# A perceiver kernel's masked cross attentions: the mask moved from TensorE to DVE and ScalarE

## The chip, the cores and the metric

The kernel runs on one core of one Trainium2 chip. The metric is the device time of one execution in microseconds; the comparison uses the median of several runs. The profile is of one further execution, taken by the hardware profiler.

## The reference, cut to what matters

The input is x, 16 batches of 64 tokens by 256, and a context of 16 x 1601 x 256. Four layers follow each other, each with a cross attention to the context, a second attention (or a scan), and a feed-forward part. Every part adds its result to x. The cross attentions of layers 1 and 3 are masked, those of layers 0 and 2 are not:

```
Q = query @ Wq + bq;  K = ctx @ Wk + bk;  V = ctx @ Wv + bv      # 16 heads of 16
scores = einsum('bhqd,bhkd->bhqk', Q, K) / 4
layer 1:  scores + mask * (-1e9)          # mask (16, 1, 1, 1601), float
layer 3:  where(mask == 0, -inf, scores)  # mask (16, 1601), int
probs = softmax(scores);  out = (probs @ V) @ Wo + bo
```

Everything is float32.

## The kernel before

The program is a sequence of stages with a barrier between them. `refresh` normalises x and projects the queries of the next cross attention; `cross_attention` then runs the attention over the context; other functions hold the other parts. There are four cross attention stages, called x0 to x3 here; in the profile their tiles all bear the name `x_`. x1 and x3 are masked.

In `cross_attention` a *unit* is one group of key tiles for one half of the heads (`c`, 8 heads) of one batch. The 1601 keys are 13 tiles of 128 (the last has 65). `GROUPS` cuts them into 4, 3, 3 and 3 tiles. A batch's context thus takes 8 cycles (`CYCLES`): two halves of the heads by four groups, and a stage has 16 x 8 = 128 cycles with scores and 8 before them. PSUM is two sets of four banks; cycle k works in set k % 2 and the maxima of cycle k are written to the other set. In cycle k, TensorE does, in this order:

- wait for the maxima of the cycle before (`max_done`), then the scores of unit k, keys on partitions (`scores`): a matmul that writes the shift (the negated maximum of every query), then 3 or 4 tiles by 4 banks of 32-row matmuls on top of it. Each bank holds four heads' worth of columns for one of four row groups.
- the scores of unit k+5 a second time with queries on partitions (`maxima`), from which DVE takes the maxima (`take_max`);
- in even cycles the weighted values of earlier units (`weigh`), into bank 0, which ScalarE must have read (`wait_exp(k, 1)`);
- the projection of one or two tiles of values four units ahead (`project_v`), into bank 0 or 1;
- in cycles with k % 4 == 3 a transpose of the maxima into bank 3 (`wait_exp(k, 4)`);
- the projection of the keys of unit k+8 (`project_k`), into bank 1 or 2.

ScalarE takes the exponents of unit k from the four banks (`exponents`), one instruction a bank, splits the context of two batches later into its high part in two cycles of a context (`split_high`), copies the turned shift (`take_shift`) and the projected keys (`take_keys`). DVE takes the maxima, then what was weighed (`take_weighed`), the values (`take_v`), and once a batch it divides and stages queries. POOL computes the low part of the context.

The mask before: `refresh` scales it and splits it into a high and a low part, and SP stores both as two rows a batch in `mask_rows`. `cross_attention` loads these two rows into four row groups of `side`, whose other rows POOL has filled with ones. A matmul over 4 rows (line 516) writes shift plus mask for each tile and bank of the scores, and one over 2 rows (line 544) the mask for each bank of the maxima. SP issues the loads: for every batch both halves of the context (`raw_in`), each after the subtraction that frees its buffer (`low_done`), then, after the last scores of the batch (`s_full`), the mask's rows of two batches later.

Of the kernel before, what the change touches and what calls it, by code (L numbers as in the profile page):

```python
# [13 lines left out]
F32 = mybir.dt.float32  # L14
# [36 lines left out]
class Net:  # L51


    def __init__(self, nc, dram, ctx):
# [11 lines left out]
        self.swap = self.sb("swap", [P, P])  # L66
# [118 lines left out]
def refresh(net, tag, add=None, query=None, xn=None):  # L185
# [3 lines left out]
             "bias_scaled q_ready m_full m_high m_low stored")  # L189
    with ExitStack() as mem, stage(nc, names) as (  # L190
            block, made, biased, added, stats_ready, var_ready, std_ready, rstd_ready, xn_ready, turned, taken, wq_in,
            mask_in, q_full, bias_scaled, q_ready, m_full, m_high, m_low, stored):
# [11 lines left out]
        if query:  # L204
# [4 lines left out]
            m_parts = net.sb(tag + "_mhl", [B, 2, CTX], F32R, ctx=mem) if mask else None  # L209
# [5 lines left out]
        if query:  # L215
            @block.sync
            def _(sp):
# [53 lines left out]
        def _(dve):  # L271
# [40 lines left out]
        def _(act):  # L312
# [10 lines left out]
            for t in range(TILES + LEAD):  # L323
# [15 lines left out]
def cross_attention(net, tag, wk, bk, wv, bv, qT, m_rows, ahead, clear=None):  # L339

    nc, d = net.nc, net.dram
    masked = m_rows is not None
    PADDED = KEY_TILES * P
    WINDOW = 48
    GROUPS = [(0, 4), (4, 7), (7, 10), (10, 13)]
# [7 lines left out]
    names = ("wv_in bias_in raw_in0 raw_in1 wk_high wk_low wv_high wv_low high_done low_done pad_set mask_in0 mask_in1 zero_set side_set shift_set "  # L353
             "sums_set q_staged m_full max_done z_step z_ready z_turned nm_ready s_full exp_done k_full k_taken v_full "
             "v_taken pv_full o_taken o_step out_ready")
    with ExitStack() as mem, stage(nc, names) as (
            block, wv_in, bias_in, raw_in0, raw_in1, wk_high, wk_low, wv_high, wv_low, high_done, low_done, pad_set, mask_in0, mask_in1,
            zero_set, side_set, shift_set, sums_set, q_staged, m_full, max_done, z_step, z_ready, z_turned, nm_ready, s_full,
# [14 lines left out]
        side = net.sb(tag + "_side", [P, 2, PADDED], F32R, ctx=mem) if masked else None  # L373
# [60 lines left out]
        def _(sp):  # L434
# [12 lines left out]
            if masked:  # L447
                sp.wait_ge(side_set, 1)
# [9 lines left out]
            for b in range(B - 2):  # L458
# [3 lines left out]
                if masked:  # L462
                    sp.wait_ge(s_full, CYCLES * b + CYCLES)
# [22 lines left out]
        def _(pe):  # L486
# [18 lines left out]
            def scores(k):  # L505
# [6 lines left out]
                if masked:  # L512
                    for t in range(lo, hi):
                        for j in range(4):
                            r = slice(32 * j, 32 * j + 4)
                            nc.tensor.matmul(mine[j][:, (t - lo) * P:(t - lo + 1) * P], side[r, u, t * P:(t + 1) * P],
                                             nm[r, c], start=(t == lo), stop=True, skip_group_check=(t > lo))
                else:
                    for j in range(4):
                        r = slice(32 * j, 32 * j + 4)  # L520
# [2130 lines left out]
```

## Time and profile before

| | |
|---|---|
| median of 3 runs | 4475.74 us (4473.22 to 4480.47) |
| the profiled execution | 4455.4 us, span 4453.6 us |
| TensorE matmul / weight load | 3800.3 us (85%) / 2972.4 us (67%) |
| DVE | 2224.7 us (50%) |
| ScalarE | 1781.0 us (40%) |
| POOL | 684.8 us (15%) |
| granted TensorE clock, mean | 0.919 of 2.4 GHz |
| DMA | 330.29 MB, mean 74 GB/s |

Busy shares are of the span. PE is TensorE's matmuls, PEld its weight loads (they overlap the matmuls), ACT is ScalarE, SP the engine that issues the loads. The instructions are named by their line in the kernel, by the tile written and the tiles read. "Idle before" is the time in which the engine stood still just before an instruction, and the releaser is what ended that wait; "issue" means that the engine waited for nothing that the profile shows.

### The profile page before, as it was taken

How to read it: one execution, taken by the hardware profiler on the slowest of the kernel's cores; microseconds unless marked ns; L12 is line 12 of the kernel's file. 1: busy time of each engine (PE TensorE's matmuls, PEld its weight loads, DVE VectorE, ACT ScalarE, POOL GpSimd, SP SyncE). 2: the span in 40 equal slices, each digit the busy share in tenths (PEclk: the TensorE clock that was granted, in tenths of full speed). 3: DMA queues.
4: the chain of work that ended last, by engine and by line, in shares of the span. 5: the costliest groups of instructions: out<-in, count | busy, mean ns of one | idle time of the engine just before them, and what ended most of it. 6: DMA issues, size and time to landing. Idle time of an engine off the chain costs nothing. (4 is left out here: it accounts for less than half of the span.)

```text
span 4453.6 us, 141607 instructions
## 1 busy us (share of the span) xinstructions
PE 3800.3 (85%) x64078; PEld 2972.4 (67%) x64078; DVE 2224.7 (50%) x4259; ACT 1781.0 (40%) x3676; POOL 684.8 (15%) x393
## 2 busy tenths in 40 slices
PE   7999998647992799999966889999963789999988
PEld 5777776525771588888725568777843678878865
DVE  4555554542443555555564355555544255555543
ACT  4555453211220345454413345555531244544431
POOL 1111110031005111111140011111112111111100
PEclk9999999668996899999987899999976899999998
DMA  3121210026994211111040111111013611010001
GB/s 102 51 84 58 68 60 12 8 102 241 352 351 133 62 47 35 47 37 45 3 114 2 32 60 47 40 40 47 18 27 140 207 53 48 33 48 33 34 11 33
DMA packets 109045, 330.29 MB, mean 74 GB/s; under 512 B 31680, under 2 KB 55760, under 8 KB 101632
## 3 DMA queue, kind: packets, MB, share of 16 engines
q1 hardware_dynamic: 98800, 299.61, 20.0%
q0 software_dynamic: 6912, 18.88, 1.3%
q8 instruction: 507, 8.31, 0.8%
q10 hardware_dynamic: 2736, 2.75, 0.2%
q14 instruction: 90, 0.74, 0.1%
HBM read 261.80 MB, written 51.00 MB: 70 GB/s over the span
## 5 line engine op out<-in xcount | busy, mean ns | idle before, releaser
L636 DVE TENSOR_REDUCE x_pm<-banks 128x4 f32<-128x1536 f32 (+2 forms) x512 | 935.6, 1827 | 1034.7 <-PE banks L547 1034.7
L759 ACT ACTIVATE x_kT<-banks,x_bk 128x384 f32<-128x384 f32 (+2 forms) x512 | 305.1, 596 | 915.1 <-PE banks L589 915.1
L744 ACT ACTIVATE x_pe<-banks 128x512 f32<-128x512 f32 (+1 forms) x1024 | 474.2, 549 | 194.2 <-PE banks L527 194.2
L576 PE MATMUL banks<-x_wh,x_ch 128*128 128x256 f32 (+1 forms) x1664 | 523.6, 315 | 9.7 <-issue 5.8
L482 POOL TENSOR_TENSOR x_cl<-xnT,x_ch 128x1601 fp32r<-128x1601 f32 x60 | 218.6, 3643 | 1769.5 <-ACT x_ch L749 1769.5
L744 ACT ACTIVATE x_pl<-banks 128x384 f32<-128x384 f32 x1024 | 419.8, 496 | 166.9 <-PE banks L527 166.9
L576 PE MATMUL banks<-x_wh,x_cl 128*128 128x256 f32 (+1 forms) x1664 | 470.3, 283 | 1.7 <-issue 1.6
L527 PE MATMUL banks<-x_q,x_kT 32*128 32x128 f32 x13312 | 470.9, 274 | 0.5 <-issue 0.5
L576 PE MATMUL banks<-x_wl,x_ch 128*128 128x256 f32 (+1 forms) x1664 | 468.5, 282 | 1.7 <-issue 1.5
L576 PEld LDWEIGHTS banks<-x_wh,x_ch 128*128 128x128 f32 (+1 forms) x1664 | 307.9, 185 | 206.1 <-ACT x_pl L744 94.4
L547 PE MATMUL banks<-x_kT,x_q 32*128 32x384 f32 (+2 forms) x4096 | 434.7, 497 | 11.3 <-ACT x_kT L759 4.5
L527 PEld LDWEIGHTS banks<-x_q,x_kT 32*128 32x128 f32 x13312 | 427.0, 182 | 3.1 <-issue 0.8
L589 PE MATMUL banks<-x_ch,x_wh 128*128 128x384 f32 (+2 forms) x1024 | 370.9, 362 | 45.0 <-DVE x_cl L730 43.9
L669 DVE TENSOR_TENSOR x_v<-banks,x_bv 128x256 f32<-128x256 f32 (+1 forms) x832 | 320.4, 417 | 171.5 <-PE banks L576 171.2
L589 PE MATMUL banks<-x_ch,x_wl 128*128 128x384 f32 (+2 forms) x1024 | 358.8, 350 | 0.0
L589 PE MATMUL banks<-x_cl,x_wh 128*128 128x384 f32 (+2 forms) x1024 | 358.2, 350 | 0.0
L576 PEld LDWEIGHTS banks<-x_wl,x_ch 128*128 128x128 f32 (+1 forms) x1664 | 309.3, 186 | 2.8 <-issue 2.8
L576 PEld LDWEIGHTS banks<-x_wh,x_cl 128*128 128x128 f32 (+1 forms) x1664 | 309.2, 186 | 1.7 <-issue 1.7
L561 PEld LDWEIGHTS banks<-x_pl,x_v 128*32 128x32 f32 (+1 forms) x12288 | 182.4, 110 | 114.4 <-ACT x_pe L744 78.0
L561 PEld LDWEIGHTS banks<-x_pe,x_v 128*32 128x32 f32 x14336 | 206.8, 110 | 75.9 <-ACT x_pl L744 69.4
L561 PE MATMUL banks<-x_pe,x_v 128*32 128x64 f32 x14336 | 228.8, 220 | 15.0 <-issue 5.0
L561 PE MATMUL banks<-x_pl,x_v 128*32 128x64 f32 (+1 forms) x12288 | 206.1, 221 | 40.4 <-issue 24.9
(371 smaller groups left out, 5538.6 us busy)
## 6 DMA issues: line engine op xcount, KB each, us to landing
e_w<-in_L_pack SPq DMA_DIRECT2D x127, 608.0 KB, 6.6
xnT<-in_ctxT SPq DMA_DIRECT2D x64, 800.5 KB, 4.4
x_raw<-in_ctxT SPq DMA_DIRECT2D x60, 800.5 KB, 5.8
e_w<-in_L_pack SPq DMA_DIRECT2D x21, 1154.0 KB, 7.5
routed_x<-x_zero SPq DMA_DIRECT2D x16, 1024.0 KB, 8.3
e_xt<-routed_x SPq DMA_DIRECT2D x16, 1024.0 KB, 8.0
routed_y<-e_y SPq DMA_DIRECT2D x32, 512.0 KB, 7.5
a_swap<-a_raw SPq DMA_DIRECT2D x64, 128.0 KB, 2.3
```

The costliest lines, as they stand in the source:

```text
L482: nc.gpsimd.tensor_tensor(cl[:, b % 2, k, 0:CTX], staged(b, k), ch[:, b % 2, k, 0:CTX], ALU.subtract).then_inc(low_done, 1)
L527: last = nc.tensor.matmul(mine[j][0:n, (t - lo) * P:(t - lo + 1) * P], kT[r, c, t * P:t * P + n], qb[r, u, c], start=False, stop=True, ski ...
L547: last = nc.tensor.matmul(into[j][:, 0:hi - lo], qb[r, u, c], kT[r, c, lo:hi], start=not masked, stop=True, skip_group_check=masked)
L561: last = nc.tensor.matmul(bank[32 * j:32 * j + 32, e * S:(e + 1) * S], v[0:w, u, t, at:at + 32], probabilities(j, t, t + 1)[0:w, 0, e * S: ...
L576: last = nc.tensor.matmul(bank[0:w, (t - lo) * D:(t - lo + 1) * D], x[:, u, c, t * P:t * P + w], y[:, 1, c, :], start=(c == m == 0), stop= ...
L589: last = nc.tensor.matmul(bank[:, 0:hi - lo], w[:, 0, i, c * P:(c + 1) * P], x[:, u, i, lo:hi], start=(i == n == 0), stop=(i == KC - 1 and ...
L636: nc.vector.tensor_reduce(pm[:, c, :, g], net.quads[1 - k % 2][:, :, 0:hi - lo], AX.X, ALU.max).then_inc(max_done, 1)
L669: ins = nc.vector.tensor_tensor(heads, bank[0:w, (t - lo) * D:(t - lo + 1) * D].rearrange("p (h e f) -> p h e f", e=2, f=16), bvb[0:w].rea ...
L744: nc.scalar.activation(probabilities(j, lo, hi).rearrange("p t q -> p (t q)"), sets[k % 2][j][:, 0:(hi - lo) * P], ACT.Exp).then_inc(exp_d ...
L759: nc.scalar.activation(kT[:, c, lo:hi], sets[k % 2][key_bank(k)][:, 0:hi - lo], ACT.Identity, bias=col[:, c:c + 1]).then_inc(k_taken, 1)
```

## The change

In the masked stages the mask no longer passes through TensorE. The scores are made as in the unmasked stages. For the maxima, SP loads one row of the mask, spread over all 128 partitions, into `shade`, and DVE adds it while it takes the maximum: four `tensor_tensor_reduce` (one a bank) in place of one `tensor_reduce`; the sums go to a new tile `added`, which nothing reads. For the exponents, the mask is laid out with keys on partitions (`m_cols`), scaled once a stage, and given as the bias of the exponents. Since a bias is one value a partition, each key tile needs its own instruction: banks 0 and 1 by tile, banks 2 and 3 together by tile. `GROUPS` becomes 3, 4, 3, 3 in the masked stages. `refresh` no longer splits the mask, `side` and its fill go, and the mask's load waits for the last maxima of a batch in place of the last scores. A tile `swap` that nothing used is no longer loaded.

```diff
@@ load_all
-            sp.dma_start(net.swap[:], d["swap16"]).then_inc(loaded, 16)
-            sp.wait_ge(loaded, 80)
+            sp.wait_ge(loaded, 64)
@@ refresh, SP
                 if mask:
-                    sp.wait_ge(m_high, 1)
-                    sp.wait_ge(m_low, 1)
-                    sp.dma_start(query.m_rows, m_parts[:].bitcast(F32)).then_inc(stored, 16)
+                    sp.wait_ge(m_full, 1)
+                    sp.dma_start(query.m_rows, m[:]).then_inc(stored, 16)
@@ refresh, DVE and ScalarE
-                if mask:
-                    dve.wait_ge(m_high, 1)
-                    nc.vector.tensor_tensor(m_parts[:, 1], m[:], m_parts[:, 0], ALU.subtract).then_inc(m_low, 1)
...
-                if mask and t == MASK_AT + LEAD:
-                    act.wait_ge(m_full, 1)
-                    nc.scalar.activation(m_parts[:, 0], m[:], ACT.Copy).then_inc(m_high, 1)
@@ cross_attention
-    GROUPS = [(0, 4), (4, 7), (7, 10), (10, 13)]
+    GROUPS = [(0, 3), (3, 7), (7, 10), (10, 13)] if masked else [(0, 4), (4, 7), (7, 10), (10, 13)]
...
-        side = net.sb(tag + "_side", [P, 2, PADDED], F32R, ctx=mem) if masked else None
+        shade = net.sb(tag + "_shade", [P, 2, CTX], ctx=mem) if masked else None
+        m_cols = net.sb(tag + "_mcols", [P, B, KEY_TILES], ctx=mem) if masked else None
+        added = net.sb(tag + "_added", [P, 4, 4 * P], ctx=mem) if masked else None
@@ SP
             def load_masks(b, u):
-                rows = m_rows[bass.ds(b, 1)].rearrange("o r n -> r (o n)")
-                for j in range(4):
-                    sp.dma_start(side[32 * j:32 * j + 2, u, 0:CTX].bitcast(F32), rows).then_inc(mask_in[u], 16)
+                sp.dma_start(shade[:, u], spread(m_rows[b:b + 1], (P, CTX))).then_inc(mask_in[u], 16)
...
             if masked:
-                sp.wait_ge(side_set, 1)
+                raw_cols = m_cols[:].rearrange("p b t -> p (b t)")
+                sp.dma_start(raw_cols.bitcast(I32) if mask == "mask_int" else raw_cols, d[mask + "_cols"]).then_inc(cols_in, 16)
                 load_masks(0, 0)
                 load_masks(1, 1)
...
                 if masked:
-                    sp.wait_ge(s_full, CYCLES * b + CYCLES)
+                    sp.wait_ge(max_done, CYCLES * b + CYCLES)
                     load_masks(b + 2, b % 2)
@@ POOL
-            if masked:
-                nc.gpsimd.memset(side[:].bitcast(F32), 1.0).then_inc(side_set, 1)
@@ TensorE, scores
-                if masked:
-                    for t in range(lo, hi):
-                        for j in range(4):
-                            r = slice(32 * j, 32 * j + 4)
-                            nc.tensor.matmul(mine[j][:, (t - lo) * P:(t - lo + 1) * P], side[r, u, t * P:(t + 1) * P],
-                                             nm[r, c], start=(t == lo), stop=True, skip_group_check=(t > lo))
-                else:
                     (the matmul of line 521, now for all stages)
@@ TensorE, maxima
-                if masked:
-                    even = hi + hi % 2
-                    for j in range(4):
-                        r = slice(32 * j, 32 * j + 2)
-                        nc.tensor.matmul(into[j][:, 0:even - lo], ones_r[r], side[r, u, lo:even], start=True, stop=True)
@@ DVE, take_max
+                if masked and c == 0 and g == 0:
+                    dve.wait_ge(mask_in[b % 2], 16 * (b // 2) + 16)
                 dve.wait_ge(m_full, unit + 1)
-                nc.vector.tensor_reduce(pm[:, c, :, g], net.quads[1 - k % 2][:, :, 0:hi - lo], AX.X, ALU.max).then_inc(max_done, 1)
+                if masked:
+                    if unit:
+                        dve.wait_ge(max_done, unit)
+                    for j in range(4):
+                        ins = nc.vector.tensor_tensor_reduce(added[:, j, 0:hi - lo], sets[1 - k % 2][j][:, 0:hi - lo], shade[:, b % 2, lo:hi],
+                                                             1.0, -3.4e38, ALU.add, ALU.max, pm[:, c, j, g:g + 1])
+                    ins.then_inc(max_done, 1)
+                else:
+                    (the tensor_reduce as before)
@@ DVE, before the cycles
+            if masked:
+                dve.wait_ge(cols_in, 16)
+                raw_cols = m_cols[:].bitcast(I32) if mask == "mask_int" else m_cols[:]
+                ops = (0.0, -3e38, ALU.is_equal, ALU.mult) if mask == "mask_int" else (-1e9, None, ALU.mult)
+                nc.vector.tensor_scalar(m_cols[:], raw_cols, *ops).then_inc(cols_ready, 1)
@@ ScalarE, exponents
+                if masked:
+                    for first, count in ((0, 1), (1, 1), (2, 2)):
+                        banks = slice(first, first + count)
+                        for t in range(lo, hi):
+                            into = first_p[:, banks, t] if t < FIRST else second_p[:, banks, t - FIRST]
+                            ins = nc.scalar.activation(into, net.quads[k % 2][:, banks, (t - lo) * P:(t - lo + 1) * P], ACT.Exp,
+                                                       bias=m_cols[:, k // CYCLES, t:t + 1])
+                        ins.then_inc(exp_done, count)
+                    return
@@ ScalarE, before the cycles
+            if masked:
+                act.wait_ge(cols_ready, 1)
```

The host lays out `mask_f32_cols` and `mask_int_cols`, the same masks padded to 13 tiles with keys on partitions.

## Rows read from the trace of the kernel before

**Rows 1.** Busy time by engine (PE, PEld, DVE, ACT, POOL), clock, DMA share, GB/s; in x1:

```profile
1550.00:2150.00 600.00, 590.63 (x12912) 487.43 (x12907) 324.25 (x558) 300.04 (x598) 89.62 (x27) 1.00 0.11 40
```

**Rows 2.** Timeline, PE: first instruction of cycles, x1 then x2; line 641 in x1, x2, x3:

```profile
1794.72 0.56 PE L516 MATMUL banks<-x_nmT,x_side 4*128 4x128 f32 x12
...
1838.08 0.56 PE L516 MATMUL banks<-x_nmT,x_side 4*128 4x128 f32 x12
...
2741.59 0.45 PE L521 MATMUL banks<-x_nmT,x_ones 4*128 4x384 f32 x4
...
2782.66 0.45 PE L521 MATMUL banks<-x_nmT,x_ones 4*128 4x384 f32 x4
...
L641 DVE TENSOR_REDUCE x_nm<-x_pm x32: 169/169/170, 1509.3 to 2192.3; 128x4 f32<-128x16 f32 x32
...
L641 DVE TENSOR_REDUCE x_nm<-x_pm x32: 169/170/170, 2601.1 to 3240.5; 128x4 f32<-128x16 f32 x32
...
L641 DVE TENSOR_REDUCE x_nm<-x_pm x32: 169/170/170, 3589.8 to 4276.6; 128x4 f32<-128x16 f32 x32
```

**Rows 3.** Timeline of three unmasked cycles (start, length, engine, line), x2:

```profile
2746.99 0.45 PE L521 MATMUL banks<-x_nmT,x_ones 4*128 4x384 f32 x4
...
2748.89 0.39 PE L576 MATMUL banks<-x_wh,x_ch 128*128 128x256 f32 x1
...
2751.51 0.50 PE L521 MATMUL banks<-x_nmT,x_ones 4*128 4x512 f32 x4
...
2752.99 2.06 ACT L744 ACTIVATE x_pe<-banks 128x512 f32<-128x512 f32 x4 [0.83 <-PE banks L527]
...
2755.94 0.39 PE L589 MATMUL banks<-x_ch,x_wh 128*128 128x512 f32 x1
...
2757.42 0.45 PE L521 MATMUL banks<-x_nmT,x_ones 4*128 4x384 f32 x4
...
2758.61 1.64 ACT L744 ACTIVATE x_pe<-banks 128x384 f32<-128x384 f32 x4 [0.40 <-PE banks L527]
...
2759.15 0.38 PE L576 MATMUL banks<-x_wh,x_ch 128*128 128x256 f32 x1
...
2761.79 0.45 PE L521 MATMUL banks<-x_nmT,x_ones 4*128 4x384 f32 x4
```

**Rows 4.** ScalarE: two timeline rows with a bias column; group of line 744 (busy, mean ns):

```profile
3451.52 1.14 ACT L1908 ACTIVATE e_h<-banks,e_w 128x128 f32<-128x128 f32 x4 [2.59 <-PE banks L1800]
...
4399.84 2.42 ACT L2396 ACTIVATE act_f<-banks,lf_b 128x512 f32<-128x512 f32 x4 [12.16 <-PE banks L2327]
...
L744 ACT ACTIVATE x_pe<-banks 128x384 f32<-128x384 f32 x512 | 209.8, 496 | 74.1 <-PE banks L527 74.1
```

**Rows 5.** Groups by line of DVE; an accumulator's read on ScalarE (ns min/median/max):

```profile
L636 DVE TENSOR_REDUCE x_pm<-banks 128x4 f32<-128x2048 f32 x128 | 293.5, 2293 | 326.0 <-PE banks L547 326.0
...
L669 DVE TENSOR_TENSOR x_v<-banks,x_bv 128x256 f32<-128x256 f32 x768 | 299.5, 418 | 171.5 <-PE banks L576 171.2
...
L1286 ACT ACTIVATION_READ_ACCUMULATOR a_s<-a_s,a_nm x8: 185/186/188, 4330.4 to 4348.6; 128x1 f32 x8
```

**Rows 6.** Around one stall in x1: SP's timeline, busy time as in rows 1, PE's timeline:

```profile
1780.28 0.43 SPq L436 DMA_DIRECT2D x_raw<-in_ctxT  x1
...
1782.00:1784.00 2.00, 2.00 (x59) 1.81 (x61) 0.74 (x3) 0.58 (x2) 0.00 (x0) 1.00 1.02 416
...
1787.69 0.39 PE L576 MATMUL banks<-x_wh,x_ch 128*128 128x256 f32 x1 [1.51 <-issue]
```

**Rows 7.** Timeline at the start of x1 and of x2:

```profile
1476.71 2.91 DVE L717 CAST x_ones<-ones 128x128 fp32r<-128x128 f32 x1 [2.69 <-PEq L44]
...
1489.97 0.69 ACT L759 ACTIVATE x_kT<-banks,x_bk 128x512 f32<-128x512 f32 x1 [6.70 <-PE banks L589]
...
2571.59 1.52 DVE L717 CAST x_ones<-ones 128x128 fp32r<-128x128 f32 x1 [2.68 <-PEq L44]
...
2582.62 0.69 ACT L759 ACTIVATE x_kT<-banks,x_bk 128x512 f32<-128x512 f32 x1 [4.49 <-PE banks L589]
```

More of the change, by code:

```diff
@@ L65, in __init__ @@
         self.eps = self.sb("eps", [P, 1])
-        self.swap = self.sb("swap", [P, P])
         self.qT = self.sb("qT", [P, KC, TOK])
@@ L336, in _, with cross_attention @@
                                          scale=0.25, bias=scaled[:, 0:1]).then_inc(q_ready, 1)
-def cross_attention(net, tag, wk, bk, wv, bv, qT, m_rows, ahead, clear=None):
+def cross_attention(net, tag, wk, bk, wv, bv, qT, mask, m_rows, ahead, clear=None):
     nc, d = net.nc, net.dram
-    masked = m_rows is not None
-    PADDED = KEY_TILES * P
+    masked = mask is not None
     WINDOW = 48
-    GROUPS = [(0, 4), (4, 7), (7, 10), (10, 13)]
+    GROUPS = [(0, 3), (3, 7), (7, 10), (10, 13)] if masked else [(0, 4), (4, 7), (7, 10), (10, 13)]
     KEYS = [(lo * P, min(hi * P, CTX)) for lo, hi in GROUPS]
@@ L535, in maxima @@
                     pe.wait_ge(q_staged, 2 * b + 2)
-                    if masked:
-                        pe.wait_ge(mask_in[u], 32 * (b - u) + 64)
                     pe.wait_ge(k_taken, CYCLES * b + 1)
                 lo, hi = KEYS[g]
-                if masked:
-                    even = hi + hi % 2
-                    for j in range(4):
-                        r = slice(32 * j, 32 * j + 2)
-                        nc.tensor.matmul(into[j][:, 0:even - lo], ones_r[r], side[r, u, lo:even], start=True, stop=True)
                 for j in range(4):
                     r = slice(32 * j, 32 * j + 32)
-                    last = nc.tensor.matmul(into[j][:, 0:hi - lo], qb[r, u, c], kT[r, c, lo:hi], start=not masked, stop=True,
-                                            skip_group_check=masked)
+                    last = nc.tensor.matmul(into[j][:, 0:hi - lo], qb[r, u, c], kT[r, c, lo:hi], start=True, stop=True)
                 last.then_inc(m_full, 1)
@@ L623, in _ @@
             pe.wait_ge(pad_set, 2)
-            pe.wait_ge(shift_set, 2 + masked)
+            pe.wait_ge(shift_set, 2)
             pe.wait_ge(sums_set, 2)
@@ L634, in take_max @@
                 lo, hi = KEYS[g]
+                if masked and c == 0 and g == 0:
+                    dve.wait_ge(mask_in[b % 2], 16 * (b // 2) + 16)
                 dve.wait_ge(m_full, unit + 1)
-                nc.vector.tensor_reduce(pm[:, c, :, g], net.quads[1 - k % 2][:, :, 0:hi - lo], AX.X, ALU.max).then_inc(max_done, 1)
+                if masked:
+                    if unit:
+                        dve.wait_ge(max_done, unit)
+                    for j in range(4):
+                        ins = nc.vector.tensor_tensor_reduce(added[:, j, 0:hi - lo], sets[1 - k % 2][j][:, 0:hi - lo], shade[:, b % 2, lo:hi],
+                                                             1.0, -3.4e38, ALU.add, ALU.max, pm[:, c, j, g:g + 1])
+                    ins.then_inc(max_done, 1)
+                else:
+                    nc.vector.tensor_reduce(pm[:, c, :, g], net.quads[1 - k % 2][:, :, 0:hi - lo], AX.X,
+                                            ALU.max).then_inc(max_done, 1)
                 if g < 3:
@@ L718, in _ @@
             nc.vector.memset(z[:].bitcast(F32), 0.0).then_inc(shift_set, 1)
-            if masked:
-                dve.wait_ge(shift_set, 2)
-                nc.vector.memset(z[:, :, 0:2].bitcast(F32), 1.0).then_inc(shift_set, 1)
             nc.vector.memset(ch[:, :, :, CTX:EVEN].bitcast(F32), 0.0).then_inc(pad_set, 1)
@@ L2456, in query, with xattn @@
             return Query(pre + "Wq", pre + "bq", pre + "Wk", mask, m_rows)
-        def xattn(layer, wo, bo, masked, clear=None):
+        def xattn(layer, wo, bo, mask, clear=None):
             pre = f"L{layer}_xattn_"
             cross_attention(net, f"x{layer}", pre + "Wk", pre + "bk", pre + "Wv", pre + "bv", net.qT,
-                            m_rows if masked else None, (pre + wo, pre + bo), clear)
+                            mask, m_rows, (pre + wo, pre + bo), clear)
             return Add(pre + wo, pre + bo)
         refresh(net, "nx0", query=query(0))
-        out_of_cross = xattn(0, "Wo", "bo", False, routed_x)
+        out_of_cross = xattn(0, "Wo", "bo", None, routed_x)
         refresh(net, "na0", add=out_of_cross)
@@ L2545, in arrange @@
     o["mask_int"] = np.ascontiguousarray(a["mask_BxS2_ik0"])
+    for name in ("mask_f32", "mask_int"):
+        padded = np.pad(o[name], ((0, 0), (0, KEY_TILES * P - CTX)))
+        o[name + "_cols"] = np.ascontiguousarray(padded.reshape(B, KEY_TILES, P).transpose(2, 0, 1).reshape(P, -1))
     o["ident"] = np.eye(P, dtype=f)
```

24 lines of the change are left out of this document (11 added, 13 removed).

## The prediction

> **What bounds the kernel now.** I read the engines' busy time by stage first. In 600 us of the second cross attention (masked), TensorE is busy 98% of the time at a granted clock of 1.00 (2.4 GHz), DVE 54%, ScalarE 50% [rows 1]. So TensorE's order of work sets the pace, and the other engines matter by how late they release it. Next the timeline, cycle by cycle. Eight cycles of `cross_attention` make one context: 43.36 us masked (1838.08 - 1794.72), 41.07 us unmasked (2782.66 - 2741.59), both free of a stall [rows 2]. The mask therefore costs 2.29 us a context, 36.6 us in each masked stage of 16, and 73 us in all: the most that taking it off TensorE can give in steady state.
>
> Then the inside of unmasked cycles [rows 3], since the changed PE code of the masked stages is that of the unmasked ones. With three key tiles ScalarE starts its exponents 1.19 us after the cycle's start (2758.61 - 2757.42), and TensorE goes on 0.54 us later, at 1.73: it waits for the first bank's exponents (496 ns [rows 4], and 0.045 to be seen), since bank 0 receives what comes next. With four tiles ScalarE starts at 1.48 (2752.99 - 2751.51), so TensorE goes on at 1.48 + 0.60 + 0.045 = 2.13. Only behind maxima of four tiles is TensorE itself the later one, at 1.90 (2748.89 - 2746.99). The exponents are thus on the path by their first bank.
>
> **The change, part by part.** I write cycles by k modulo 4, times from a cycle's start.
>
> *Removed from TensorE:* the mask matmuls of lines 516 and 544. This gives the unmasked pace, -2.29 us a context.
>
> *Exponents.* ScalarE now makes 6 instructions of 128 columns and 3 of 256 for three tiles, 8 and 4 for four, each with a column of biases. This very form is in the trace: four 128x128 from PSUM with such a bias take 1.14 us [rows 4], 368 ns each by the line's own summary, so one starts every 0.258 us. Four of 512 columns take 2.42 us at 688 ns, one every 0.577; between the two, 256 columns start every 0.365 and last 0.475. Bank 0 is then done after 2 x 0.258 + 0.368 = 0.88 us (was 0.50), with four tiles after 1.14 (was 0.60). The whole unit takes 6 x 0.258 + 2 x 0.365 + 0.475 = 2.75 us (was 1.64), and 3.63 (was 2.06).
>
> *The groups.* The four-tile group's exponents move from k=0 to k=1, its maxima from k=3 to k=0, its keys' projection from k=0 to k=1. Six matmuls of 512 columns instead of 384 cost 0.34 us more: projecting 512 takes 1.48 (2755.94 to 2757.42), so 384 takes 1.14. Two value tiles take 2.64 - 1.14 = 1.50, where 2.64 is 2761.79 - 2759.15.
>
> The cycles against the unmasked ones, TensorE going on 0.045 us after an exponent's end:
> - k=0: 1.19 + 0.88 + 0.045 = 2.12, against 2.13. Keys 384 instead of 512: **-0.35**, so 5.91 (2757.42 - 2751.51) becomes 5.55.
> - k=1: 1.48 + 1.14 + 0.045 = 2.66 against 1.73, and keys +0.34: **+1.27**.
> - k=2: 2.12 against 1.74: **+0.38**.
> - k=3: values start at 2.12 and end at 3.62, but the transpose needs bank 3, free at 1.19 + 2.75 + 0.045 = 3.98. Before, it came at 1.90 + 1.50 = 3.40: **+0.58**.
>
> That is +1.88 in four cycles, +3.76 a context. Less the 2.29 it is +1.47 a context, times 16 contexts and 2 stages: **+47 us**. ScalarE's load itself is no bound: 3 x 2.75 + 3.63 and about 4.3 for keys, shift and split are 16 us of about 22.
>
> *Maxima on DVE.* Four TENSOR_TENSOR_REDUCE in place of one reduction (2293 ns for 4 x 512 [rows 5]). The trace has none. Below: no less than the one reduction, 2.3 us. The nearest row, an addition of 256 columns from PSUM, takes 418 ns; the reduction's 2293 ns over 2048 columns and this leave 1.05 ns a column and 0.15 us fixed. With all of it serial, 512 columns take 0.69 and four 2.75. Above: an accumulator's read behind each at ScalarE's 186 ns gives 3.5 us [rows 5]. The room is, in k=0, 5.55 less a start near 2.05 and 0.17 for the release, 3.3 us; in k=3, 5.1 - 1.85 - 0.17 = 3.1 for 384 columns (2.2 to 2.9). I take it as hidden by the exponents and projections, since only the upper end of k=0 passes, by 0.2 us; 0 to 0.2 x 32 x 2 = 13 us for the range. Uncovered, every 0.1 us costs 6 us. Queued behind it on DVE are the weighed sums and values of the cycle, needed only at the next cycle's maxima.
>
> The Trainium skill, "VectorE: DVE Perf Modes", section "Two Vector instructions with no wait between them", speaks against this part: an op that writes its accumulator is two instructions. No row here shows it on DVE; it would take the sum to the upper end just given, not beyond it.
>
> "ScalarE: Activation LUTs" (the Trainium skill, section "What ACT_TABLE_LOAD costs") gives 280 + 0.833N ns with a pointer bias and 93 ns of overlap: 0.294 us from start to start at 128 columns, where rows 4 show 0.258. By it a context would be about 2.7 us longer than before, +87 us before the savings below. The measured row decides.
>
> *Loads.* SP's order matters here. Before, SP waited for the last scores of a context, issued the mask rows, then both context loads together: the second at 1780.28, the DMA engines are full (1.02) at 1782 to 1784, and at 1787.69 TensorE starts after 1.51 us in which it waited for nothing the profile shows [rows 6]. That its instructions come late is my reading. How much this is in all, line 641 tells, which runs once in half a context: 32 times from 1509.3 to 2192.3, 15.5 contexts of 44.06 us, and 44.31 in the other masked stage, against the 43.36 without a stall: 11 and 15 us, 26 together. The unmasked stage has 41.25 against 41.07, 3 us, with the same two loads a context, but one at a time. After the change the mask (128 x 6.4 KB, as much as one context load) goes out behind the maxima in k=2 and both context loads follow at about k=5 and 7, all three apart. Three lone loads would cost 3 x 1.5 = 4.5 us a stage, 9 for both: **-17 us**. The bounds are 0 and -26.
>
> *Start of a stage.* POOL's fill of the side rows goes, beside which DVE's first copy took 2.91 us instead of 1.52. The first keys are copied 13.3 us after that copy's start (1489.97 - 1476.71), unmasked 11.0 (2582.62 - 2571.59) [rows 7]: -2.2 each. The five cycles before the first scores lose mask matmuls of about 2.29 / 8 = 0.28 each. Together 2 x (2.2 + 1.4): **-7**. The mask's high and low parts in `refresh` go too; that is uncounted, under 1 us a stage, since the other tiles' work goes on beside it. The new columns of the mask (106 KB) and their one DVE operation lie under the split of the value weights; if that cover were gone they would cost under 1 us a stage. The missing load of `swap` lies beside x's 1 MB.
>
> Sum: +47 - 17 - 7 = **+23 us**. The profiled execution took 4455.4 us (span 4453.6), 0.45% under the median of the runs, 4475.74; I carry the difference over: 4499 us.
>
> **Rivals.**
> 1. *As above*, own range 4486 to 4514, chance 0.45.
> 2. *The stalls vanish altogether*, and a little of each cycle with them: 47 - 26 - 7 = +14, 4490; with 0.01 us less in the exponents' start-to-start time (10 us, see 5) it is +4, 4480, no change by 0.2% (9 us, about what a measurement can tell). For it: stalls come beside paired loads. Against: lone loads leave some. Chance 0.2, over half of it within 0.2%.
> 3. *The mask's loads make stalls of their own*, nothing saved: 47 - 7 = +40, 4516; with one more of 1.5 us every second context, 24 us, 4540. Each context moves 0.8 MB more. Chance 0.1.
> 4. *DVE becomes the bound*: at half a column's rate, 512 columns four times take 4.9 us, k=0 is 7.1 us instead of 5.55, k=3 0.5 longer: 2 us x 64 = 130 us, 4630; with only 0.3 us too much in k=0 and k=3, +38, 4537. Against: every other DVE row runs a column a cycle. Chance 0.13.
> 5. *Faster*: the small exponents overlap more than rows 4 show. Each 0.01 us off the start-to-start time is worth about 10 us, so from 0.226 on the kernel is faster by over 0.2%. At 0.17, which is what exponents without bias show (0.381 for 384 columns), the context is 1.35 us shorter than before: 4476 - 43 - 24 = 4409. The same sign comes if exponents start earlier than I take. Chance 0.12.
>
> **How the numbers follow.** Likeliest 4499. The range 4462 to 4550 leaves out the deeper part of case 5 and the far part of case 4, under 2 in 10. Faster 0.12; same: the larger part of case 2 and the edges of cases 1 and 5, 0.2; slower 0.68.
>
> **What would show it.** In the changed trace: eight masked cycles of about 44.8 us; cycles of 5.55, 5.67, 5.8 and 5.1 us; TensorE's weight loads idle before line 576 or 561 by up to a microsecond on ScalarE's exponents; 128x128 exponents at 368 ns; no idle before TensorE's first scores that ends with DVE. Fewer waits of TensorE that nothing shown ends. The prediction falls if a masked context is below 43.4 us, or if DVE's maxima end the cycles.

## The result and the profile after

| | before | after |
|---|---|---|
| median of 4 runs, us | 4477.57 (4473.22 to 4480.47) | 4511.24 (4510.42 to 4513.4) |
| ratio, 95% interval | 1 | 1.0075 [1.0059, 1.009] |
| profiled execution, its span | 4455.4, 4453.6 | 4511.7, 4509.9 |
| x1, x3: start to end | 740.7, 742.7 | 757.1, 758.5 |
| x1, x3: one context | 44.06, 44.31 | 44.93, 44.97 |

The change makes the kernel 33.7 us slower, inside the range and 12 us above the forecast. The two profiled executions lie 56 us apart, of which only 32.2 us are in the masked stages x1 and x3. The rest lies in code that the change doesn't touch: 29.7 us more between x0 and x1, where the routed experts work, 5.6 us less in x0. The profile of before is 22 us under the median of its own runs, and it is the odd one: its x1 begins 1476.7 us into the kernel, that of every other profile, a4 and b1 with the old `refresh` among them, between 1494.7 and 1507.7. So from here on stages are compared with stages, and kernels by ratios of medians.

First the busy time of the same 600 us of x1, columns as in [rows 1], and the line of `negmax`, which takes the negated maxima once in half a context (line 625 now, 641 before), in x1 and x3, all of the kernel after:

```profile
1550.00:2150.00 600.00, 552.26 (x11350) 439.07 (x11353) 343.58 (x1287) 425.61 (x1200) 86.33 (x26) 1.00 0.17 57
...
L625 DVE TENSOR_REDUCE x_nm<-x_pm x32: 169/170/172, 1531.4 to 2227.8; 128x4 f32<-128x16 f32 x32
...
L625 DVE TENSOR_REDUCE x_nm<-x_pm x32: 169/170/172, 3630.7 to 4327.7; 128x4 f32<-128x16 f32 x32
```

TensorE was 98% busy [rows 1]; now it is 92%, and ScalarE has gone from 50 to 71%. (2227.8 - 1531.4) / 15.5 is the 44.93 us of the table: the mask matmuls have gone, and the context is longer. The waits of the same stretch say why (us in total, times, longest):

```profile
PEld banks L549 <- ACT x_pe L734: 32.3, 26, 1.2
...
PEld banks L534 <- ACT x_pe L734: 26.5, 27, 1.0
PEld banks L549 <- ACT x_pl L734: 26.5, 27, 1.0
PEld banks L534 <- ACT x_pl L734: 26.2, 27, 1.0
...
PEld banks L589 <- ACT x_pl L734: 11.2, 27, 0.5
```

TensorE's values (549), weighing (534) and the transpose (589) wait for ScalarE's new exponents (734), once in every cycle. In this stretch none of TensorE's waits of any size ends with line 615, DVE's maxima, and none above 0.4 us is left that nothing shown ended; the middle of x3 has none either, where before there were such as in [rows 6]. One cycle with four key tiles and the one behind it, PE, ScalarE and DVE from the timeline of after:

```profile
1701.55 0.51 PE L502 MATMUL banks<-x_nmT,x_ones 4*128 4x512 f32 x4
...
1703.03 3.63 ACT L734 ACTIVATE x_pe<-banks,x_mcols 128x128 f32<-128x128 f32 x12 [0.78 <-PE banks L508]
1703.67 0.56 DVE L615 CUSTOM_DVE_ANT_0 x_added<-banks,x_shade 128x384 f32<-128x384 f32 x1 [2.57 <-PE banks L521]
1704.16 0.08 DVE L615 DVE_READ_ACCUMULATOR2_ANT x_pm<- 128x1 f32 x1
1704.16 0.55 DVE L615 CUSTOM_DVE_ANT_0 x_added<-banks,x_shade 128x384 f32<-128x384 f32 x1
1704.22 0.39 PE L549 MATMUL banks<-x_wh,x_ch 128*128 128x256 f32 x1 [0.62 <-ACT x_pe L734]
...
1705.59 0.08 DVE L615 DVE_READ_ACCUMULATOR2_ANT x_pm<- 128x1 f32 x1
...
1707.22 0.45 PE L502 MATMUL banks<-x_nmT,x_ones 4*128 4x384 f32 x4
...
1708.41 2.76 ACT L734 ACTIVATE x_pl<-banks,x_mcols 128x128 f32<-128x128 f32 x9 [0.40 <-PE banks L508]
...
1709.35 1.77 PE L534 MATMUL banks<-x_pe,x_v 128*32 128x64 f32 x112 [0.46 <-ACT x_pl L734]
```

ScalarE starts 1.48 us into the cycle, TensorE goes on at 2.67 (1704.22 - 1701.55), the cycle is 5.67 long, all as worked out for k=1, and the twelve exponents take the 3.63 us and the nine 2.76 that were forecast. DVE is done at 4.12 (1705.67). The median cycles of k=1, 2, 3, 0 are 5.67, 5.79 (6.49 with two value tiles), 5.15 and 5.58 us, forecast 5.67, 5.8 (6.47), 5.1 and 5.55. Eight of them make 45.07 us in the middle of the stage, and the mean is the median: there are no stalls.

### The profile page after: what moved, and what is told of

Its sections match the earlier page's. It is cut to its first block and busy times, and to the rows that moved or that the text cites. A ratio compares the mean times of both kernels' runs of the same rounds, so it can differ in the third digit from the quotient of the medians.

```text
span 4509.9 us, 138366 instructions
## 1 busy us (share of the span) xinstructions
PE 3750.2 (83%) x60750; PEld 2885.1 (64%) x60750; DVE 2279.7 (51%) x6049; ACT 2094.2 (46%) x5146; POOL 676.8 (15%) x391
## 3 DMA queue, kind: packets, MB, share of 16 engines
q10 hardware_dynamic: 2736, 2.75, 0.2%
## 5 line engine op out<-in xcount | busy, mean ns | idle before, releaser
L615 DVE CUSTOM_DVE_ANT_0 x_added<-banks,x_shade 128x384 f32<-128x384 f32 (+2 forms) x1024 | 527.3, 571 | 533.8 <-PE banks L521 476.1
L619 DVE TENSOR_REDUCE x_pm<-banks 128x4 f32<-128x1536 f32 (+2 forms) x256 | 467.8, 1827 | 473.8 <-PE banks L521 473.8
L508 PE MATMUL banks<-x_q,x_kT 32*128 32x128 f32 x13312 | 458.6, 270 | 0.0
L734 ACT ACTIVATE x_pe<-banks,x_mcols 128x128 f32<-128x128 f32 (+1 forms) x1344 | 409.3, 430 | 91.4 <-PE banks L508 91.3
L508 PEld LDWEIGHTS banks<-x_q,x_kT 32*128 32x128 f32 x13312 | 445.3, 183 | 5.0 <-issue 0.2
L734 ACT ACTIVATE x_pl<-banks,x_mcols 128x128 f32<-128x128 f32 (+1 forms) x1152 | 353.0, 425 | 62.9 <-PE banks L508 62.9
L739 ACT ACTIVATE x_pe<-banks 128x512 f32<-128x512 f32 (+1 forms) x512 | 237.1, 549 | 85.8 <-PE banks L508 85.8
```

The costliest lines, as they stand in the source:

```text
L508: last = nc.tensor.matmul(mine[j][0:n, (t - lo) * P:(t - lo + 1) * P], kT[r, c, t * P:t * P + n], qb[r, u, c], start=False, stop=True, ski ...
L615: ins = nc.vector.tensor_tensor_reduce(added[:, j, 0:hi - lo], sets[1 - k % 2][j][:, 0:hi - lo], shade[:, b % 2, lo:hi], 1.0, -3.4e38, ALU ...
L619: nc.vector.tensor_reduce(pm[:, c, :, g], net.quads[1 - k % 2][:, :, 0:hi - lo], AX.X, ALU.max).then_inc(max_done, 1)
L734: ins = nc.scalar.activation(into, net.quads[k % 2][:, banks, (t - lo) * P:(t - lo + 1) * P], ACT.Exp, bias=m_cols[:, k // CYCLES, t:t + 1])
L739: nc.scalar.activation(probabilities(j, lo, hi).rearrange("p t q -> p (t q)"), sets[k % 2][j][:, 0:(hi - lo) * P], ACT.Exp).then_inc(exp_d ...
```

## The experiments

Eleven kernels ran, each beside the kernel before on the same chip. The chip was not the same one for all, and the median of the kernel before was 4479.2 us beside a1 to a4, 4484.1 beside b1 to b4 and 4476.4 beside c1 to c3, so the ratios are what can be compared. The masked context is (last - first) / 15.5 of the line of `negmax`, in x1 and x3.

| run | edit | median, us | ratio, 95% | context x1, x3 |
|---|---|---|---|---|
| a1 | after, exponents by bank, no mask in them | 4375.5 | 0.9776 [0.9761, 0.979] | 41.12, 41.14 |
| a2 | after, groups 4, 3, 3, 3 | 4528.2 | 1.011 [1.0095, 1.0126] | 45.37, 45.63 |
| a3 | after, mask load behind the scores | 4522.1 | 1.01 [1.0085, 1.0116] | 45.10, 45.41 |
| a4 | before, loads apart | 4454.9 | 0.9945 [0.9931, 0.996] | 43.54, 43.46 |
| b1 | a4, no mask in the maxima | 4430.3 | 0.9886 [0.9868, 0.9904] | 42.47, 42.66 |
| b2 | after, a fifth maximum | 4511.7 | 1.0068 [1.0051, 1.0084] | 44.87, 44.92 |
| b3 | after, fewer exponents in k=3 | 4482.6 | 1.0 [0.9991, 1.001] | 44.11, 44.16 |
| b4 | after, mask in the values | 4383.6 | 0.977 [0.9751, 0.979] | 41.48, 41.55 |
| c1 | a1 with a3's loads | 4404.4 | 0.9842 [0.9829, 0.9855] | 41.79, 42.01 |
| c2 | after, plain maxima | 4503.6 | 1.0065 [1.0053, 1.0077] | 44.78, 44.83 |
| c3 | b4, other product | 4392.3 | 0.982 [0.9805, 0.9835] | 41.97, 42.20 |

**a1, the exponents undone.**

```diff
                 act.wait_ge(s_full, k + 1)
-                if masked:
+                if False:
                     for first, count in ((0, 1), (1, 1), (2, 2)):
```

> The changed kernel with one part undone: in the masked cross attentions the exponents are again one instruction a bank, without a bias, so that the mask is left out of the exponents (it still goes into the maxima). Theory (the exponents by tiles are the whole cost in steady state): the masked cycles fall to the unmasked pace, 45.07 us a context to about 41.1, and the end of the stages loses its 5.5 and 6.8 us: 4511 - 31 x 4.0 - 12 = about 4375 us. Rival (DVE's maxima or the order of the groups hold the pace too): a context stays above 42.5 us, the kernel above 4420 us.

4375.5 us, 3.81 and 3.83 us less a context, and x1 from start to end 65.8 us shorter (757.1 to 691.3), of which 15.5 x 3.81 = 59 is pace. The exponents by tiles cost 3.0% of the kernel (1.0075 less 0.9776), four times the change's whole loss; DVE's four masked maxima and the groups stay in this kernel and don't hold it above the unmasked 41.07 us [rows 2] by more than 0.1. The run takes away two things at once, the number of instructions and their bias. That the number counts, b3 shows; no run keeps the small instructions and drops the bias.

**a2, the groups alone.**

```diff
-    GROUPS = [(0, 3), (3, 7), (7, 10), (10, 13)] if masked else [(0, 4), (4, 7), (7, 10), (10, 13)]
+    GROUPS = [(0, 4), (4, 7), (7, 10), (10, 13)]
```

> The changed kernel with the key groups 4, 3, 3, 3 in the masked stages too. Theory (each cycle is its TensorE work behind the bank that it waits for): by the prediction's own steps k=0 gains 0.53 us, k=1 0.39, k=2 0.38, k=3 0.58 over unmasked ones, 1.88 in four cycles as with 3, 4, 3, 3: the time stays at 4511 us, within 5. Rival (DVE's four maxima of 512 columns now lie in k=3, where the value projection and the transpose end late, and they end the cycle): k=3 grows by 0.2 us or more, and the kernel is 13 us slower or more.

Some 16 us slower than the changed kernel (1.011 / 1.0075), and neither theory had the reason. Its k=3 takes the same 5.14 us, with DVE's four tiles in it; k=0 takes 6.76 where 6.44 was worked out. The timeline of a2, k=0:

```profile
1713.91 0.50 PE L502 MATMUL banks<-x_nmT,x_ones 4*128 4x512 f32 x4
...
1715.39 3.63 ACT L734 ACTIVATE x_pe<-banks,x_mcols 128x128 f32<-128x128 f32 x12 [0.84 <-PE banks L508]
...
1718.76 0.28 PE L549 MATMUL banks<-x_wl,x_ch 128*128 128x256 f32 x1
1719.07 0.19 PEld L562 LDWEIGHTS banks<-x_ch,x_wh 128*128 128x128 f32 x1 [0.24 <-ACT x_pe L734]
```

In k=0 TensorE also weighs, so the keys' projection goes to bank 2, which is free only when all twelve exponents are done: 1715.39 + 3.63 = 1719.02, and TensorE starts at 1719.07. That wait is 0.24 of the 0.32 us. In the changed kernel the four tiles are in k=1, where the keys go to bank 1. So the change's groups are worth 16 us to it, by the bank and not by DVE. The sum in the expectation had given the regrouping nothing either way; for k=0 it had counted the first bank alone.

**a3 and a4, the loads.** a3 is the changed kernel with SP's order of before; a4 is the kernel before with only that order changed:

```diff
# a3
-                    sp.wait_ge(max_done, CYCLES * b + CYCLES)
+                    sp.wait_ge(s_full, CYCLES * b + CYCLES)
# a4
-                for k in range(KC):
-                    sp.wait_ge(low_done, 2 * b + k + 3)
-                    load_context(b + 2, k)
-                if masked:
-                    sp.wait_ge(s_full, CYCLES * b + CYCLES)
-                    load_masks(b + 2, b % 2)
+                sp.wait_ge(low_done, 2 * b + 3)
+                load_context(b + 2, 0)
+                if masked and b >= 1:
+                    sp.wait_ge(s_full, CYCLES * b)
+                    load_masks(b + 1, (b - 1) % 2)
+                sp.wait_ge(low_done, 2 * b + 4)
+                load_context(b + 2, 1)
```

> The changed kernel, with the mask's load waiting for the last scores of a context, as before, instead of the maxima; both context loads are then issued together behind it. Theory (TensorE's stalls came with two context loads issued together): the stalls come back, 11 and 15 us, and the kernel takes about 4537 us (4525 to 4545). Rival (the stalls came with the mask matmuls' own instructions on TensorE, which are gone either way): no stall, 4511 us within 5.

> The kernel before with only the order of SP's loads changed: the mask rows of a context are issued between the two context loads, so that these go out one at a time, about two cycles apart, as in the unmasked stages. Theory (stalls come with paired context loads): a masked context falls from 44.06 and 44.31 us to about 43.4, the kernel by some 26 us, to about 4451 us (4447 to 4462). Rival (the stalls belong to the mask matmuls' instructions): no change, 4477 us within 5.

a4 takes 24 us off the kernel before by moving its two context loads apart (the mask's rows stay just ahead of the second), and its context is 43.54 and 43.46 us, close to the 43.36 without a stall. SP's queue in a4, where [rows 6] had both context loads at once:

```profile
1703.86 0.36 SPq L436 DMA_DIRECT2D xnT<-in_ctxT  x1
1714.19 1.14 SPq L441 DMA_DIRECT2D x_side<-mask_rows  x4
1715.38 0.36 SPq L436 DMA_DIRECT2D x_raw<-in_ctxT  x1
```

a3 gives the stalls back to the changed kernel, but only 11 us of them (9.5 by the contexts), not 26. That needed one more run.

**c1, the same loads without the waits on exponents.** a1 and a3 together, so no new lines.

> The run a1 (bank exponents, the mask left out of them; 4375 us) with the mask's load behind the last scores as in a3, so that a mask load and both context loads go out together once a context. The run a3 gave back only 11 us of the 26 that paired loads had cost before. Theory (the transfers make TensorE's instructions late by so much whatever it does, and in a3 its waits for the small exponents absorbed most of it): with the waits short again 20 to 26 us come back, about 4398 (4392 to 4404). Rival (the stalls need the dense small mask matmuls in TensorE's stream, 1,400 more instructions in 600 us, which neither kernel has): 10 us or less, 4375 to 4386.

29 us over a1 (23.9 by the contexts). One of its stalls, SP and then PE of c1:

```profile
1663.76 0.33 SPq L430 DMA_DIRECT2D x_shade<-mask_rows  x1
1664.13 0.43 SPq L427 DMA_DIRECT2D xnT<-in_ctxT  x1
1664.61 0.43 SPq L427 DMA_DIRECT2D x_raw<-in_ctxT  x1
...
1673.91 0.61 PE L508 MATMUL banks<-x_q,x_kT 32*128 32x128 f32 x13 [0.68 <-issue]
```

So loads issued together make TensorE late in a kernel without a single mask matmul, and the rival falls. With the same loads, the kernel that waits on ScalarE in every cycle shows less of it: 11 us in a3 against 29 here. That those waits absorb the lateness, and that it is the instructions that come late, stays my reading; the runs show when it happens and what it costs, not what is late.

**b1, the maxima's half.** The mask matmuls ahead of the maxima go, out of a4:

```diff
-                if masked:
-                    even = hi + hi % 2
-                    for j in range(4):
-                        r = slice(32 * j, 32 * j + 2)
-                        nc.tensor.matmul(into[j][:, 0:even - lo], ones_r[r], side[r, u, lo:even], start=True, stop=True)
...
-                    last = nc.tensor.matmul(into[j][:, 0:hi - lo], qb[r, u, c], kT[r, c, lo:hi], start=not masked, stop=True,
-                                            skip_group_check=masked)
+                    last = nc.tensor.matmul(into[j][:, 0:hi - lo], qb[r, u, c], kT[r, c, lo:hi], start=True, stop=True)
```

> The kernel before with its loads apart (the run a4) and the mask out of the maxima alone: the mask matmuls on TensorE ahead of the maxima go, and the maxima are taken over all keys, masked ones too (any shift that is not below the largest masked score gives the same softmax); the mask still enters the scores by TensorE, and the exponents are one instruction a bank. Theory (the maxima's half of the change pays by itself, the exponents' half costs): the mask matmuls ahead of the maxima took 0.23 to 0.31 us eight times a context, 2.1 us, of which the wait for the first bank's exponents takes back up to 1.2: a context of 42.0 to 42.5 us, the kernel 30 to 45 us under a4's 4455, about 4417. Rival (the exponents' release already bounds the cycle, so nothing on TensorE ahead of it pays): 4455 within 8.

25 us under a4, where the theory had 30 to 45: 1.07 and 0.80 us a context of the 2.1 that those matmuls took. Some 0.7 us of the rest goes into waiting for ScalarE's exponents, sooner reached: those waits of TensorE's weight loads make 62.7 us of 600 in a4 and 73.5 in b1. The mask in the scores costs TensorE about 1.4 us a context, from b1's 42.47 and 42.66 to the unmasked stage of b1's own trace, 41.16 (a1, which differs from b1 in its groups and maxima too, has 41.1). The change replaces that by 3.8 us of waits on the exponents.

**b2 and c2, DVE's part enlarged and taken out.**

```diff
# b2, behind the four of a unit
+                    nc.vector.tensor_tensor_reduce(twice[:, 0:hi - lo], sets[1 - k % 2][3][:, 0:hi - lo], shade[:, b % 2, lo:hi],
+                                                   1.0, -3.4e38, ALU.add, ALU.max, spare[:, unit % 2:unit % 2 + 1]).then_inc(max_done, 1)
# c2, in place of the four, and no load_masks
+                nc.vector.tensor_reduce(pm[:, c, :, g], net.quads[1 - k % 2][:, :, 0:hi - lo], AX.X,
+                                        ALU.max).then_inc(max_done, 1)
```

> The changed kernel with a fifth tensor_tensor_reduce behind the four of each masked unit (the last bank once more; results of the additions are written as bfloat16 to find room, they are never read). It adds 0.475 us on DVE at 384 columns and 0.61 at 512. Theory (DVE is covered by more than that): four of 512 end 4.58 us into their cycle of 5.67, with a fifth 5.19, and the release takes under 0.2: the time stays 4511 us within 6. Rival (DVE is close to the bound, its values and weighed sums behind the maxima are late for the next cycle): 0.3 us or more in k=1 or k=0, four units a context, 20 us or more.

> The changed kernel with the other half undone: maxima are one plain reduction a unit over all keys, masked ones too (same softmax while the largest score of all is not some 87 above the largest that counts), and no mask rows are loaded in the stage; the exponents by tiles and the groups 3, 4, 3, 3 stay. Theory (DVE's share of the change and its 0.8 MB loads are hidden): 4511 us, less up to 5 at the stages' start. Rival (they cost something in the pace): a masked context of 44.95 us falls by 0.3 us or more, 4501 or below.

With a fifth maximum the time is the same (4511.7). Without any, and without the mask's loads, it is some 4 us less, inside what the intervals can tell; the contexts say 0.15 us each, 4.5 us. So in the middle of a stage DVE is not the bound and has at least the 0.4 to 0.6 us of a fifth maximum to spare in each cycle, and rivals 3 and 4 are out.

**b3, the exponents cheaper where the last bank counts.**

```diff
-                    for first, count in ((0, 1), (1, 1), (2, 2)):
+                    for first, count in (((0, 1), (1, 3)) if k % 4 == 3 else ((0, 1), (1, 1), (2, 2))):
```

> The changed kernel, with the exponents of banks 1, 2 and 3 in one instruction of 384 columns a tile in k=3 alone (6 instructions in place of 9). Theory (in k=3 TensorE waits for the last bank before the transpose, at 4.00 us): from the start-to-start times 0.258, 0.365 and 0.577 at 128, 256 and 512 columns, 384 take about 0.47, so the unit ends 0.45 us sooner, and the transpose is then bound by the values, at 3.62: k=3 goes from 5.15 to about 4.8, twice a context: 4511 - 2 x 32 x 0.36 = about 4488. Rival (the transpose waits for something else, DVE's chain of the shift, ready near 4.1): 4511 within 5.

k=3 falls from 5.15 to 4.74 us, and the kernel by 0.75% (1.0 / 1.0075), to the time of before. That is some 34 us; k=3 alone gives 2 x 32 x 0.41 = 26 of them, and the two masked stages of the profiles are 29 us shorter. PE and ScalarE in k=3 of b3:

```profile
1705.29 0.45 PE L502 MATMUL banks<-x_nmT,x_ones 4*128 4x384 f32 x4
1706.48 2.30 ACT L734 ACTIVATE x_pl<-banks,x_mcols 128x128 f32<-128x128 f32 x6 [0.50 <-PE banks L508]
...
1708.93 0.27 PE L589 MATMUL banks<-ident,x_z 128*128 128x128 f32 x1
```

The unit takes 2.30 us instead of 2.75, and the transpose comes at 3.64, with nothing before it to wait for, where it was 4.00. The step "k=3" of the prediction is confirmed by taking its cause away.

**b4 and c3, the mask in the values.** Softmax's factor exp(mask) is one number for each key, so it can be put on the key's row of values and on its columns of ones, instead of on 1,024 exponents:

```diff
+                    dve.wait_ge(v_taken, n + 1)
+                    for t in range(lo, hi):
+                        w = P if t < KEY_TILES - 1 else LAST_KEYS
+                        ins = nc.vector.tensor_scalar(v[0:w, u, t], plain[0:w, t - lo], m_cols[0:w, n // CYCLES, t:t + 1], None, ALU.mult)
+                    ins.then_inc(v_scaled, 1)
```

> The mask in another place: cross attention as the unmasked stages have it (groups 4, 3, 3, 3, plain maxima over all keys, exponents by bank, no load of mask rows), and each tile of values with its columns of ones is multiplied by exp(mask) of its keys, a column for each tile: one more DVE instruction of 384 columns for each of 13 tiles a context, 0.3 to 0.45 us each, 4 to 6 us of 41. Softmax is the same as long as the largest score of all keys is not some 87 above the largest of the keys that count. Theory (DVE has the room, and it is off the path): the pace of the run a1 (4375 us), less some us at the start of the stages: 4370 (4360 to 4382). Rival (the products are late for the weighing two cycles a context, or for the release of the bank): 0.3 us twice a context and more, 4395 or above.

> The run b4 (mask in the values) with the product of values and mask column as a tensor_tensor with a column read over and over instead of a tensor_scalar. In b4 (4384 us, 41.5 us a context against 41.1 in a1) this product took 0.42 us, but 3.6 to 3.85 once a context and 1.95 for two once a context, each time while POOL's subtraction of 3.67 us ran, while the additions from PSUM beside it kept 0.42. Theory (any instruction of DVE that reads two operands in SBUF is held while POOL works, a port is shared): held as before, 4384 to 4392 with some 0.14 us more each. Rival (only tensor_scalar is held): no product above 1 us, 41.15 us a context, 4373.

b4 is 100 us faster than before and about 3% faster than the changed kernel, the best of all that compute the reference. (Its maxima, exponents and groups are those of the unmasked stages, and no mask rows are made or loaded. What is new is in the diff, and ScalarE takes exp of the mask's columns once a stage.) Its context is 0.4 us above a1's, and the timeline of b4 shows where from:

```profile
1725.94 3.67 POOL L464 TENSOR_TENSOR x_cl<-xnT,x_ch 128x1601 fp32r<-128x1601 f32 x1 [28.50 <-ACT x_ch L732]
...
1725.99 3.85 DVE L649 TENSOR_SCALAR x_v<-x_plain,x_mcols 128x384 f32<-128x384 f32 x1
```

A product that takes 0.42 us elsewhere takes 3.85 while POOL subtracts, the maxima behind it end late, and the next cycle takes 4.72 us (median) where the same cycle of the unmasked stage in b4's trace takes 4.38. c3's form, a `tensor_tensor` with both operands in SBUF, takes 0.56 us and is held in the same way (4.03), so it is slower still, as the theory had it. The weight of this for the change itself is nil: its maxima read one operand in PSUM, and in 600 us of x1 52 of them ran beside POOL, all of 384 columns and none above 0.56 us.

## Why the prediction held, step by step

- *Which way, and the mechanism*: right. Exponents by tiles free the first bank late, TensorE waits for it, and that costs more than the mask matmuls did. a1 shows it alone.
- *Exponents, +47*: measured +49. By the first and last of line 625 it is (44.93 - 43.36) x 15.5 and (44.97 - 43.36) x 15.5, 1.59 us a context against the 1.47 forecast. Each cycle was right within 0.1 us, since 128 and 512 columns had rows of their own form [rows 4] and 256 lay between the two. (43.36 is the pace in the middle of a stage, while 44.93 and 44.97 are means over all of it, and these lie 0.1 below the middle's 45.07 without a stall. Middle against middle it is 1.71 us a context: an estimate of +53 us for the exponents, and then of -30 for the stalls below. Their sum stays.)
- *Maxima on DVE, 0*: right in the middle of the stages (b2, c2). The trace has 0.55 us at 384 columns, 0.69 at 512, one starting 0.48 and 0.61 us behind the other, the same slope as the estimate, and an accumulator's read of 0.08 us, at once with the start of the next. Four of 512 end 4.58 us into k=0, which takes 5.58. The rule of the Trainium skill ("VectorE: DVE Perf Modes", "Two Vector instructions with no wait between them") that such an op is two instructions agrees with these rows; its price was less than half the 186 ns that I took as the upper bound from ScalarE.
- *Stalls, -17*: the right sign, too small. No stall is left, -26 us. The step that failed is "three lone loads would cost 3 x 1.5 = 4.5 us a stage". It took one unmasked stage's 3 us for a price of a lone load. a4 shows loads apart to take off most of it in the old kernel, 24 us. That TensorE's long waits on the exponents absorb the remainder would be the obvious reason, but a1 speaks against it: its waits are short, its three loads go out apart as in the changed kernel, and in its masked stages the cycles that lie over 0.15 us above their median add up to 0.3 and 0.5 us, against 3.8 in the unmasked stage of the same trace. All the kernels with groups 3, 4, 3, 3 and loads apart (after, a1, b2, b3, c2) have under 1 us a masked stage by this count, those with 4, 3, 3, 3 (a2, a4, b1, b4, c3) 0 to 9. Why is open. Rival 2 had this half right; its other half, still shorter exponents, did not come.
- *Start of a stage, -7*: measured -2.5 and -1.2. The first `negmax` of x1 now comes 30.1 us after the stage's start (before 32.6), of x3 30.0 (31.2). The fill gave what was forecast: DVE's first copy takes 1.53 us, and in both stages TensorE begins to project keys after 8.2 us (before 10.3). The -1.4 for the mask matmuls of the opening cycles is the part that failed: from the first matmul of the maxima to `negmax` it is 14.8 us (before 15.1), 0.3 less. TensorE is not the bound there; it stands before the maxima's matmuls in wait for ScalarE's keys and, in the changed kernel as before, for DVE (PE of after):

```profile
1519.78 1.14 PE L521 MATMUL banks<-x_kT,x_q 32*128 32x512 f32 x8 [1.18 <-DVE x_pm L615]
1524.00 0.93 PE L521 MATMUL banks<-x_kT,x_q 32*128 32x384 f32 x8 [1.13 <-DVE x_v L653]
```

  And x3 lost 1.2 us between the two, in the projection of keys. Before, the granted clock rose there from 1.2 to 2.4 GHz sooner than in x1; now it doesn't. That stretch of x3, before and then after, columns as in [rows 1] (the sixth figure behind the comma, ahead of the DMA share, is the clock):

```profile
3568.89:3574.71 5.82, 5.10 (x19) 4.23 (x20) 0.45 (x1) 1.85 (x3) 0.00 (x0) 0.74 0.64 209
```

```profile
3608.88:3615.88 7.00, 6.28 (x19) 5.41 (x19) 0.64 (x2) 1.85 (x3) 0.00 (x0) 0.60 0.99 404
```

  In x1 it is 0.57 and 0.59. When the clock rises at a stage's start varies between the runs, and what sets it they don't show.
- *End of a stage*: not in the sum at all, +5.6 and +6.8. From the last `negmax` to the end x1 takes 30.7 us (before 25.1), x3 31.5 (24.7); with the exponents by bank (a1) it is 7.0 and 7.7 us less than in the changed kernel. The last cycles project nothing, so nothing covers any bank's exponents. ScalarE at the end of x1, after, then before:

```profile
2239.86 3.64 ACT L734 ACTIVATE x_pe<-banks,x_mcols 128x128 f32<-128x128 f32 x12 [2.71 <-PE banks L508]
2243.30 2.84 ACT L734 ACTIVATE x_pl<-banks,x_mcols 128x128 f32<-128x128 f32 x9
2247.21 2.75 ACT L734 ACTIVATE x_pl<-banks,x_mcols 128x128 f32<-128x128 f32 x9 [1.07 <-PE banks L508]
```

```profile
2202.53 1.64 ACT L744 ACTIVATE x_pe<-banks 128x384 f32<-128x384 f32 x4 [1.42 <-PE banks L527]
2204.03 1.67 ACT L744 ACTIVATE x_pl<-banks 128x384 f32<-128x384 f32 x4
2207.65 1.64 ACT L744 ACTIVATE x_pl<-banks 128x384 f32<-128x384 f32 x4 [1.95 <-PE banks L527]
```

  There is no work left for either set to hide behind, and the last three units, one of them of four tiles now, take 9.23 us where they took 4.95.

The terms as measured: +49 - 26 - 4 + 12 = +31, against +32.2 between the stages and +33.7 between the medians. Against the forecast's +23 the end of the stages adds 12, the start 3 and the exponents 2, and the stalls take off 9. That the forecast came within 12 us of the result is in part luck: the ends of the stages, which were not in the sum, and the stalls that all vanished are errors of about 10 us each with opposite signs. The mechanism and the size of its main term are not.

## What to carry to other kernels

An engine at half load can still set the pace: what counts is how soon it frees the first buffer that the bound engine needs, and splitting an instruction into small ones, each with its own bias, delays that first release (0.88 against 0.50 us here, and 3.63 against 2.06 for the last). Price each half of a change against the kernel's own cycle, with the cycles at a stage's start and end on their own, where nothing covers what the middle hides and another engine can be the bound. And before work is moved from one engine to another, ask whether it can be applied where there is less of it: the mask on 13 tiles of values cost 0.4 us a context, in the scores and exponents 1.4 by TensorE or 3.8 by ScalarE.

## What the runs showed of the hardware that was not expected

- Two or three loads of 0.8 MB issued within a microsecond cost this kernel 24 to 29 us in all (a4, c1); the same bytes 10 us and more apart cost little (under 1 us a masked stage in a1). TensorE, which none of them feeds at that moment, pauses in some of the contexts (in x1 of the kernel before in every second one) for 0.7 to 2.6 us and goes on 8 to 10 us after the first of the loads is issued.
- A DVE product that reads only SBUF stands still while POOL subtracts in SBUF: as `tensor_scalar` it takes 3.85 us instead of 0.42, as `tensor_tensor` 4.03 instead of 0.56, beside a POOL instruction of 3.67, while DVE's additions from PSUM keep their 0.42. The Trainium skill's "GPSIMD Engine Reference", section "Specifications", has the interfaces to SBUF shared, with contention for instructions in a two-port mode or with two inputs in SBUF; c3, whose product has two inputs in SBUF, agrees, at a hold about as long as POOL's instruction; b4's `tensor_scalar` is held for as long, and its trace doesn't say in which mode it ran.
- `tensor_tensor_reduce` from PSUM with float32 output and with bfloat16 output (b2) takes the same 0.55 us at 384 columns.
